# A fused two-layer-feed-forward and attention kernel on one core: u turned by block transposition and DRAM copies in four batches, and the order tables that go with it

## The reference

```python
def ffn(x):
    h = LN(x) * ln_gamma + ln_beta
    return x + 0.5 * (silu(h @ w1 + fc1_bias) @ w2 + fc2_bias)      # 128 -> 512 -> 128

def attention(x):                                                    # 16 heads of 8
    q, k, v = split(x @ w_qkv)
    w = relu(q @ k.T / sqrt(8))
    out = (w / (sum(w) + 1e-6)) @ v
    return LN(x + out @ w_out + b_out) * gamma + beta

x = x + 0.5 * ffn(LN(x))
x = x + attention(LN(x))
return x + 0.5 * ffn(LN(x))
```

## Time and profile before

| | us |
|---|---|
| median of 3 runs (lowest, highest) | 357.94 (357.79, 358.27) |
| the profiled execution | 357.93 |
| its span, first to last instruction | 356.0 |
| PE busy | 345.8 (97%) |
| DVE busy | 261.6 (73%) |
| ACT busy | 221.4 (62%) |
| POOL busy | 220.2 (62%) |

### The profile page before, as it was taken

How to read it: one execution, slowest core, us unless ns; L and a number is a source line. 1 busy time by engine, 2 the same in 40 slices (tenths; PEclk the granted TensorE clock), 3 DMA queues, 4 the chain that set the end, 5 groups by cost and what they waited for, 6 DMA issues and landing times.

```text
span 356.0 us, 12686 instructions
## 1 busy us (share of the span) xinstructions
PE 345.8 (97%) x4958; PEld 154.6 (43%) x4958; DVE 261.6 (73%) x658; ACT 221.4 (62%) x396; POOL 220.2 (62%) x469
## 2 busy tenths in 40 slices
PE   8989999999999999999999999999999999999986
PEld 6732523522346333553335423553335533532365
DVE  4757557875788876988678886788748976678773
ACT  3377577577764667556774567556674557677623
POOL 7598186089955799169964699258942784036441
PEclk9999999999999999999999999999999999999999
DMA  7017115510632136422362126311380024500001
GB/s 215 10 49 178 47 31 133 158 38 5 148 90 87 36 91 141 99 63 90 76 165 61 33 90 155 85 61 43 85 201 6 2 90 98 142 31 1 4 4 61
DMA packets 22027, 28.49 MB, mean 80 GB/s; under 512 B 3408, under 2 KB 10320, under 8 KB 21968
## 3 DMA queue, kind: packets, MB, share of 16 engines
q1 hardware_dynamic: 19376, 23.60, 25.8%
q10 hardware_dynamic: 2592, 4.07, 3.7%
HBM read 6.43 MB, written 4.98 MB: 32 GB/s over the span
## 4 chain that ended last, share of the span: by engine, by line
PE 89%; POOL 3%; DVE 3%; issue 2%; ACT 2%; DMA 1%; POOLq 0%; DVEq 0%; ACTq 0%
PE o_bank L801 33%; PE scores L778 15%; PE pre_bank L716 11%; PE pre_bank L709 10%; PE post_bank L709 8%; PE post_bank L716 6%; PE scores L716 3%; PE pre_bank L701 1%; POOL u L1409 1%; ACT probs L1076 1%; DMA pre_x<-in_x_dram 1%; POOL norm_x_rs L1381 1%; PE o_bank L695 1%; POOL norm_x_rs L1396 0%; POOL post_h L1409 0%
## 5 line engine op out<-in xcount | busy, mean ns | idle before, releaser
L1076 ACT ACTIVATE probs<-scores 128x512 f32<-128x512 f32 x276 | 148.4, 597 | 73.6 <-PE scores L778 71.9
L1348 DVE TENSOR_SCALAR probs<-scores 128x512 f32<-128x512 f32 x223 | 143.2, 678 | 46.4 <-PE scores L778 44.3
L801 PE MATMUL o_bank<-probs,v_op 128*32 128x512 f32 x1024 | 136.0, 603 | 0.9 <-ACT probs L1076 0.4
L778 PE MATMUL scores<-q_op,k_op 32*128 32x512 f32 x499 | 67.7, 495 | 0.4 <-DVE q_op L1285 0.4
L778 PEld LDWEIGHTS scores<-q_op,k_op 32*128 32x128 f32 x499 | 26.4, 181 | 70.7 <-issue 55.3
L1378 POOL TENSOR_SCALAR norm_y_var<-norm_y_mv 128x4 f32<-128x4 f32 x7 | 1.4, 198 | 64.5 <-DVE norm_y_mv L1132 64.5
L801 PEld LDWEIGHTS o_bank<-probs,v_op 128*32 128x32 f32 x1024 | 21.6, 108 | 35.0 <-issue 34.8
L709 PEld LDWEIGHTS post_bank<-w,post_y 128*32 128x32 f32 x960 | 27.1, 110 | 13.6 <-issue 12.7
L709 PEld LDWEIGHTS pre_bank<-w,pre_y 128*32 128x32 f32 x960 | 27.1, 110 | 12.7 <-issue 10.2
L709 PE MATMUL pre_bank<-w,pre_y 128*32 128x128 f32 x960 | 31.6, 273 | 0.0
L709 PE MATMUL post_bank<-w,post_y 128*32 128x128 f32 x960 | 31.0, 273 | 0.0
(11 more groups left out here) (174 smaller groups left out, 427.6 us busy)
## 6 DMA issues: line engine op xcount, KB each, us to landing
k_op<-k_parts SPq DMA_DIRECT2D x62, 128.0 KB, 2.7
q_op<-q_parts SPq DMA_DIRECT2D x62, 128.0 KB, 2.7
out_dram<-o_rows ACTq DMA_DIRECT2D x7, 256.0 KB, 2.4
pre_x<-in_x_dram ACTq DMA_DIRECT2D x6, 256.0 KB, 2.6
pre_past<-pre_blocks SPq DMA_DIRECT2D x6, 256.0 KB, 3.7
pre_t<-pre_past SPq DMA_DIRECT2D x24, 64.0 KB, 2.0
post_past<-post_blocks SPq DMA_DIRECT2D x5, 256.0 KB, 2.0
post_t<-post_past SPq DMA_DIRECT2D x20, 64.0 KB, 2.2
```

Of the source, the lines that this page charges most:

```text
L778: mm(score_bank(b, s, i, j), k_op[rows, g, P * kt:P * (kt + 1)], q_op[rows, g, :], start=True, stop=True).then_inc(scores_done[i], 1)
L801: last = mm(o_bank[pair][VW * j:VW * (j + 1), :], v_op[:, kt, heads_of(g).start + 2 * j, :], probs[:, s % 2, j, :], start=(odd == 0 and kt ...
L1076: activation(probs[:, s % 2, 2 * i + j, :], score_bank(b, s, i, j), ACT.Relu).then_inc(probs_done[i][j], 1)
L1348: v.tensor_scalar(probs[:, s % 2, 2 * i + j, :], score_bank(b, s, i, j), 0.0, None, ALU.max).then_inc(probs_done[i][j], 1)
```

## The change

**u by copies.** For batches 3 to 6 (`U_BY_DMA`) the PE task `uT` and ACT's copy are dropped. DVE turns u in blocks (a new task `u.turn`), SP writes the blocks to DRAM and reads them back into t_u, and PE waits before q, k and v until all four reads have landed. The state of such a turning becomes a class, `Turned`, which pre, post and u use. Because t_u's columns then stand in the order by quarters, the output projection of those batches takes its tokens by quarter. POOL, before it overwrites u, waits for DVE's turning instead of PE's transposes.

**SP's order.** In a loop with u: write u, write post's rows, read u, read post's rows. The pre stage's turning, now for batch b + 3, stands before the last of the four groups of k and q copies.

**New orders.** One more quarter of the first layer goes before u in loop 0 (three) and loop 1 (all four), and all four before k from loop 2 on; the second layer's first quarter of the next batch moves to the end of the loop before. x's statistics, application and turning are for batch b + 3 at the end of a loop instead of b + 2 at its start. x1 and its statistics stand in steps 3 and 4 on DVE, u before post's rows on POOL. Loop 6 gets tables of its own on ACT and DVE.

```diff
-AHEAD = {1: (["fc1.0", "fc1.1"], ["fc1.2"], ["fc1.3"]), 2: (["fc1.0", "fc1.1", "fc1.2"], ["fc1.3"], [])}
-LATER = (["fc1.0", "fc1.1"], [], ["fc1.2", "fc1.3"])
+U_BY_DMA = range(3, B - 1)
...
+        split = 4 if b == 1 else 5
+        after = [fill for fill in ("uT", "k", "q", "v") if not (fill == "uT" and b in U_BY_DMA)]
+        for fills, batch in ((PRE_FILLS[1:split], b + 1), (after, b), (PRE_FILLS[split:6], b + 1)):
...
 POOL_ORDER = [
-    "v_in.2", "post.u_bias", "pre.x_stats@2", "pre.x_apply@2", "post.y_stats@-1", "post.y_gamma@-1", "post.x2_stats@-1",
-    "post.x_apply@-1", "v_in.3", "pre.x1_stats@1", "pre.u_apply@1", "post.xr@-1", "pre.x1_beta@1", "pre.xr@2",
-    "v_in.0@1", "v_in.1@1"
+    "v_in.2", "post.u_bias", "post.y_stats@-1", "post.y_gamma@-1", "pre.x1_stats@1", "pre.u_apply@1",
+    "post.x2_stats@-1", "post.x_apply@-1", "v_in.3", "pre.xr@2", "post.xr@-1", "pre.x_stats@3", "pre.x_apply@3",
+    "v_in.0@1", "v_in.1@1", "pre.x1_beta@1"
...
-THREE_BY_ACT = {0: (7, 8, 12, 13), 1: (3, 5, 6, 10, 11), **{b: (3, 6) for b in range(2, B - 1)}, B - 1: (0, 1, 2, 3, 4, 8, 9, 10, 14)}
+THREE_BY_ACT = {0: (2, 7, 8, 12, 13), 1: (3, 5, 6, 10, 11), **{b: (3, 6) for b in range(2, B - 2)},
+                B - 2: (3, 6, 7, 10, 11), B - 1: (0, 1, 2, 3, 4, 8, 9, 10, 14)}
...
+            def send(turned, b):
+                sp.wait_ge(turned.turned, turned.turns(b))
+                sp.dma_start(turned.past, turned.blocks[:, :, :]).then_inc(turned.left, 16)
+            def fetch(turned, b, last_use):
+                sp.wait_ge(turned.left, 16 * turned.turns(b))
+                sp.wait_ge(*last_use)
+                for j in range(HG):
+                    sp.dma_start(turned.t[VW * j:VW * (j + 1), :].rearrange("c (i e) -> c i e", i=HG),
+                                 turned.past.rearrange("(i c) j e -> c i j e", i=HG)[:, :, j, :]).then_inc(turned.t_in, 16)
...
             def iteration(b):
                 n = b + 1
-                if n > 0 and n != 2 and b + 2 in pre.by_dma:
-                    turn(pre, b + 2)
+                if n == 1:
+                    turn(pre, 2)
+                if n in U_BY_DMA:
+                    send(u_by_copies, n)
                 if b - 1 in post.by_dma:
-                    turn(post, b - 1)
+                    send(post.by_copies, b - 1)
+                if n in U_BY_DMA:
+                    fetch(u_by_copies, n, (pre.full, pre.after("v", b)))
+                if b - 1 in post.by_dma:
+                    fetch(post.by_copies, b - 1, (post.full, post.after("fc1.3", b - 2)))
                 for g in range(NG):
-                    if n == 1 and g == NG - 1:
-                        turn(pre, 3)
+                    if n > 0 and g == NG - 1 and b + 3 in pre.by_dma:
+                        turn(pre, b + 3)
...
+                        if b in U_BY_DMA:
+                            pe.wait_ge(u_by_copies.t_in, TURN_DONE * u_by_copies.turns(b))
                         by_columns(pre.bank[:, :], wqk[:, i, :], t_u[:, :]).then_inc(pre.full, 1)
...
-                            last = by_tokens(post.bank, aT, t, wo[:, :], True, True)
+                            last = by_tokens(post.bank, aT, t, wo[:, :], True, True, b in U_BY_DMA)
...
+                            if b - 1 in U_BY_DMA:
+                                pool.wait_ge(u_by_copies.turned, u_by_copies.turns(b - 1))
+                            else:
+                                pool.wait_ge(pre.full, pre.after("uT", b - 1))
```

More of the change, by code:

```diff
@@ L217 @@
     [],
-    [],
     ["pre.fc1.0@2"],
     ["pre.fc1.1@2"],
-    ["post.store@-2", "pre.uT@1"],
+    ["pre.fc1.2@2"],
+    ["post.store@-2", "pre.fc1.3@2"],
     ["pre.k@1"],
@@ L224 @@
     ["post.fc1.1@-1", "pre.v@1"],
-    ["post.fc1.2@-1", "pre.fc1.2@2"],
-    ["post.fc1.3@-1", "pre.fc1.3@2"],
+    ["post.fc1.2@-1"],
+    ["post.fc1.3@-1"],
+]
+ACT_BARE = [
+    [],
+    [],
+    [],
+    [],
+    [],
+    [],
+    [],
+    [],
+    ["pre.uT@1"],
+    ["pre.k@1"],
+    ["pre.q@1"],
+    ["pre.v@1"],
+    ["post.store@-2", "post.fc1.0@-1"],
+    ["post.fc1.1@-1"],
+    ["post.fc1.2@-1"],
+    ["post.fc1.3@-1"],
 ]
@@ L303 @@
     ["pre.k_lo@1"],
+    ["pre.x_stats@3", "pre.q_lo@1"],
+    ["a.0"],
+    ["pre.turn@3"],
+    [],
+]
+DVE_BARE = [
+    ["oT.1@-1", "den.1@-1"],
+    ["a.1@-1", "aT@-1"],
+    ["post.y@-1", "post.y_stats@-1"],
+    ["pre.x1@1"],
+    ["pre.x1_stats@1"],
+    ["post.x2@-1", "post.x2_stats@-1"],
+    [],
+    [],
+    ["post.turn@-1"],
+    ["pre.k_lo@1"],
     ["pre.q_lo@1"],
+    ["post.out@-2"],
+    ["oT.0", "den.0"],
     ["a.0"],
-    ["pre.x_stats@3"],
+    [],
     [],
@@ L381, in tasks @@
         batch = b + int(offset or 0)
+        if what == "uT" and batch in U_BY_DMA or stage == "u" and batch not in U_BY_DMA:
+            continue
         if 0 <= batch < B and ((stage, batch) not in (("pre", 0), ("post", B - 1)) or what in BESIDE):
@@ L1067, in _ @@
             for b in range(B):
-                for s, beside in enumerate(of_batch(b, ACT_START, ACT_SECOND, ACT_ORDER, ACT_END)):
+                order = ACT_BARE if b == B - 2 else ACT_ORDER
+                for s, beside in enumerate(of_batch(b, ACT_START, ACT_SECOND, order, ACT_END)):
                     if STEPS * b + s - 1 > 0:
```

119 lines of the change are left out of this document (60 added, 59 removed).

## The result

The changed kernel took 360.97 us (median of 4 runs, 360.29 to 361.27) beside 358.11 (4 runs, 357.79 to 358.69) for the kernel before: ratio 1.0075, 95% interval 1.0055 to 1.0096. It is slower by 2.9 us where 354.1, faster, was predicted, and the time lies outside the range. The profiled execution took 361.13, its span is 359.3, 3.3 more than before.

A forecast was written before the change was run, and what follows sets the result against it. The prediction took PE (TensorE) to bound the kernel, its step lengths following the work given it. Its terms, -2.84 - 1.01 - 0.40 + 0.40 + 0 = -3.85, took 357.93 to 354.1 us, with an eight-in-ten range of 353.0 to 356.8.

The forecast's parts named there:

- signs named as wrong: PE idle before k or post's first layer; step 10's scores over 0.3 longer; u's read over 3.5 us after its turn.
- Term 1: Loops 2 to 5: u's four transposes leave PE, 0.71 us saved in each, -2.84 us.
- Term 2: Loops 0 and 1: a first-layer quarter ahead of u ends PE's wait for POOL's u, -1.01 us.
- Term 3: Loop 6: one bare PE step instead of two, less lost after it, -0.4 us, bounds 0 and -1.2.
- Term 4: Loops 2 to 5: DVE waits for POOL's post rows, making step 9's relus late, +0.4 us, bounds 0 and +1.6.
- Term 5: Copies through DRAM on SP's queue: u and post's rows land before PE wants them, 0 us.
- rival 3: SP's order as new bound: u's reads behind post's rows, k waits 1.76 us in four loops, 361.1 us; chance 0.13.
- rival 1: Copies a little late, slow write or longest landing: PE waits 0.4 to 0.8 per loop, 355.7 to 357.3; chance 0.15.
- Rival 2: PE not the bound, or the change does less: late relus fill term 1, 356.5 to 357.9 us; chance 0.08.

The follow-up runs named there:

- e4_all: Changed kernel with den in step 11, DVE's steps 8 and 9 exchanged, and u read before post's rows are sent: 357.60 us, 0.9983 of the kernel before.
- e9_rec: Changed kernel without den, the reciprocal reading the sums directly in its place (small constant left out): 357.68 us, 0.9978 of the kernel before.
- e2_turn: Changed kernel with DVE's steps 8 and 9 exchanged in loops 2 to 5, post's rows turned in step 9: 360.97 us, 1.0073 of the kernel before.
- e3_sp: Changed kernel with u read back on SP before post's rows are sent: 361.16 us, 1.0069 of the kernel before.
- e7_one: Changed kernel with den adding its constant as an immediate number, one operand instead of two: 360.55 us, 1.0057 of the kernel before.

## Why the prediction was wrong

PE's side of the sum held. What failed is what the sum gave to DVE, POOL and the copies: operations kept the durations that they had beside their old neighbours, though POOL's new order put other work beside them, and four reads were priced at the median of one. Three of the signs named as wrong are there: PE idle before k, scores of step 10 longer by 0.55, and u read 4.1 us after it was turned.

**Term 1** (-2.84) held: with the waits gone a loop is 0.75 shorter (e4_all). **Term 2** (-1.01) gave -0.78: loop 0 fell by 0.41, loop 1 by 0.37 without the fill it took over. PE's wait for POOL's u is gone from the list of waits.

**Term 3** (loop 6, -0.4) came out as +0.45: the loop gave up a fill of 0.86 and is only 0.41 shorter. DVE's wait for post's rows, whose price I put at 0.4, is 2.04 us long there, since the steps in front are shorter, and step 10 alone lost 0.90. Another 0.37 was `den` (e9_rec), and step 11, with 2.62, lost 0.33 where I had 0.15 for the fills on one bank.

**Term 4** (+0.4) was mis-sized: +2.2. The mechanism was the one named, DVE's wait for post's rows with the relus of step 9 queued behind it. I had post's rows at 163.65 on the clock of the earlier trace rows, 21.92 after the loop's first scores; they came 22.45 after (164.53 + 1.75 - 143.83). The 0.53 between is POOL's first operation of u's chain, 0.73 instead of 0.20, held by DVE's addition of x2. So the relus were 0.91 late, not 0.42, which is beyond their slack of 0.36 (2.29 - 1.93): 0.55 in step 10. I had written the bound (+1.6 if POOL is 0.3 later), and taken the near end of it, for a chain of POOL that I had moved to a stretch in which POOL used to stand idle (155.93 to 158.07 in the loop of the earlier trace rows), without asking what DVE did in that stretch: it added x2 (0.68 us from 155.97). POOL's wait there, in loop 3 of the kernel before:

```profile
158.07 0.20 POOL L1378 TENSOR_SCALAR norm_x_var<-norm_x_mv 128x4 f32<-128x4 f32 x1 [2.14 <-DVE norm_x_mv L1132]
```

**Term 5** (0) cost 1.3: 0.94 in loop 2 and 0.35 in loop 3. I had given u's reads a slack of 0.84, with 2.2 from issue to landing for the last of the four. That is the median of single reads, but PE waits for all four: the last one took 3.1 and 3.2 in loops 2 and 3 and 2.6 in loops 4 and 5, as the longest of the earlier trace rows, 3.1, could have told. In loop 3 that is 0.96 more than I gave it, more than the slack. The later turn of post's rows cost little by itself: u's first read came 0.55 later (23.67 after the loop's first scores instead of 23.12), but the stretched step 10 put k off by 0.52 as well, and loops 4 and 5, with their first reads at 23.66 and 23.67, did not wait. In loop 2 the reads also came later: the first at 24.19, and the four issues took 2.48 instead of 1.76. So the place is rival 3's and the kind rival 1's, reads at their longest landing. e2_turn shows what one more microsecond on DVE does: k waits in all four loops.

By the Trainium skill's rule (DMA: Bandwidth & Descriptors, Queues, rings and completion order) u's reads count as landed only after post's earlier write has landed. The traces agree in so far as no read of u landed before that write in the four loops of the changed kernel or of e2_turn. It does not explain the slow last read: in loop 3 the write lands at 169.10, and that read, issued at 168.88, at 172.05. With the write in front the reads landed in 2.2 us by the median here and in 2.7 in e2_turn, without it in 2.0 in e3_sp. What lies closer is the output store, which rival 1 names: ACT issues it 0.05 to 0.07 before the last read in loops 3 to 5, and the read lands 0.19 to 0.24 after it (172.05 after 171.86 in loop 3). No run moved the store, so this stays open.

**The term that was missing** is `den`: 1.8 us in step 12, 0.5 in loop 2, 0.37 in loop 6, about 2.7 in all, the largest single loss. The prediction gave it no row, since in loops 2 to 5 it kept its kind, its number and its place in step 10. What changed is what runs beside it: POOL no longer stands the 2.14 us for x2's statistics, so its residual comes earlier, and the residual's addition of 1.28 us begins 26.75 after the loop's first scores (pre's, 170.58) instead of 28.26 (post's, 169.99 before), while `den` begins at 26.82 instead of 26.49. In loop 6 the new table has `den` in step 12 instead of 10, and there post's addition is beside it. The addition of loop 3 before, behind `den`:

```profile
169.99 1.28 POOL L1444 TENSOR_TENSOR post_xr<-post_xr,b_quarter 128x512 f32<-128x512 f32 x1
```

The trace of before had shown the effect once, in loop 0, where it did little harm (DVE, then POOL):

```profile
60.07 0.40 DVE L1144 TENSOR_TENSOR den<-o_t,kern_eps 128x32 f32<-128x32 f32 x1
```

```profile
59.13 1.29 POOL L1493 TENSOR_TENSOR x_beta<-x,rows 128x512 f32<-128x512 f32 x1
```

`den` takes 0.40 and ends at 60.47, POOL's addition at 60.42. The Trainium skill states the rule (SBUF — State Buffer, Who interferes with whom): DVE shares its second pair of ports into SBUF with GpSimd, and whoever issues first blocks the other; a DVE operation with two operands in SBUF contends with a GpSimd operation that reads SBUF, so does one in a two-port mode, which a tensor-scalar operation can enter, and one with a single SBUF operand outside these modes does not. The traces agree in both directions: `den` went from 0.21 to 1.26 as tensor-tensor and from 0.19 to 1.26 as tensor-scalar, the reciprocal took 0.35 either way, and POOL's operation went from 0.20 to 0.73. Whether e7_one's `den` was in a two-port mode no run here shows. I had looked up the cost of what was added, not what the moved work would stand beside.

**Rival 2** (PE not the bound) is half true for the changed kernel: POOL and DVE hold a quarter of its chain, in the steps named. For the loops themselves it is false: with the waits gone they take what PE's fills take, 40.19 us (e4_all). Rival 3's 361.1 lies beside the measured 360.97 by coincidence: its wait before k is 1.3 us of the loss, not 7.0.

**The sum.** Predicted -3.85, found in the loops +2.57, a difference of 6.4, made up, step by step and rounded, of `den` 2.3 in loops 2 to 5, term 4 1.8, term 5 1.3, term 3 0.85 (with `den` in loop 6), term 2 0.2. The start adds 0.75 in this profile by chance.

Open: in loop 2 step 12 still takes 4.1 to 4.2 in every version that reads u first, with post's reads late by about 1 us. u's four issues take 2.0 to 3.0 us there and 1.7 in loops 3 to 5, and post's write behind them lands in 2.7 to 3.7 us instead of 2.1 to 2.4. Why the first loop with u's copies is slower was not tried.
